# Inverse roots on the vector engine, another order in the wide attention layers, and filled gate chains

## What is computed

```python
x = x + L0_xattn(layernorm(x), ctx, ctx)      # "raw": 16 heads of 8, causal
x = x + L0_ffn(layernorm(x))                  # "ffn0": ternary weights, GELU
x = x + L1_xattn(layernorm(x), ctx, mask)     # "rows": 16 heads of 64, row mask
x = x + L1_ffn(layernorm(x))                  # "ffn1": batch norm, product keys, top 8
x = x + L2_xattn(ctx, layernorm(x))           # "bias": 16 heads of 8, causal, biases
x = x + L2_ffn(layernorm(x))                  # "ffn2": 8 experts, the best one, GELU
x = x + L3_xattn(layernorm(x), ctx, ctx, ...) # "keys": 16 heads of 64
x = x + L3_ffn(layernorm(x))                  # "ffn3": 8 experts, best two, + 2 shared ones
# layernorm(x) = (x - mean) / sqrt(var + 1e-5)
# shared part of ffn3: sh = silu(x @ ws_gate.T) * (x @ ws_up.T) @ ws_down.T
```

## Time and profile before

| what | us |
|---|---|
| median of 3 runs (lowest to highest) | 1647.35 (1647.21 to 1652.68) |
| profiled execution | 1640.3 |
| its span | 1638.5 |
| PE busy in the span | 1413.3 (86%) |
| DVE busy | 1022.6 (62%) |
| ACT busy | 898.7 (55%) |
| Pool busy | 690.4 (42%) |

### The profile page before, as it was taken

One profiled execution on the slowest core, in us unless ns is written; L12 is line 12 of the kernel. 1 busy time (PEld: TensorE's weight loads), 2 busy tenths in 40 slices (PEclk: granted clock), 3 DMA queues, 4 the chain that ended last, 5 costly groups with the idle time before them and its releaser, 6 DMA issues.

```text
span 1638.5 us, 30033 instructions
## 1 busy us (share of the span) xinstructions
PE 1413.3 (86%) x9437; PEld 937.4 (57%) x9449; DVE 1022.6 (62%) x3380; ACT 898.7 (55%) x1867; POOL 690.4 (42%) x1056
## 2 busy tenths in 40 slices
PE   5996889999998577868778895899899999996998
PEld 2443457777766476767654443444576777664343
DVE  5653366666665799998955554433566666655444
ACT  3665456666665477777746663333566666661222
POOL 5341144444443589989853331000344444441000
PEclk9999899999999689998999997999999999997999
DMA  2016000000000000000000000000000000000000
GB/s 66 17 49 252 4 4 5 3 3 3 3 3 1 26 1 1 1 0 0 1 1 1 1 2 1 26 1 0 4 4 4 3 3 6 0 1 1 7 6 13
DMA packets 12665, 21.76 MB, mean 13 GB/s; under 512 B 3088, under 2 KB 9120, under 8 KB 11936
## 3 DMA queue, kind: packets, MB, share of 16 engines
q1 hardware_dynamic: 12576, 20.63, 3.5%
HBM read 19.58 MB, written 1.05 MB: 13 GB/s over the span
## 4 chain that ended last, share of the span: by engine, by line
PE 61%; DVE 17%; ACT 12%; issue 8%; POOL 2%; DVEq 0%; ACTq 0%; DMA 0%; SPq 0%; POOLq 0%
PE bank L932 7%; PE bank L969 6%; PE bank L947 5%; DVE sb_both L1841 4%; PE bank L919 4%; ACT sb_both L1036 4%; PE bank L1880 3%; PE bank L2060 3%; PE bank L898 3%; PE bank L409 2%; PE bank L1888 2%; PE bank L451 2%; PE bank L1889 2%; PE bank L899 2%; PE bank L2130 2%
## 5 line engine op out<-in xcount | busy, mean ns | idle before, releaser
L1213 POOL TENSOR_TENSOR sb_both<-sb_both,sb_winv 128x512 f32<-128x512 f32 x256 | 260.8, 1040 | 323.7 <-DVE sb_winv L1143 323.7
L1036 ACT ACTIVATE sb_both<-sb_both,sb_wneg 128x256 f32<-128x256 f32 x512 | 253.0, 495 | 151.0 <-DVE sb_wneg L1137 150.9
L1768 POOL TENSOR_TENSOR sb_KM<-sb_OT 128x1024 f32<-128x1024 f32 x128 | 240.2, 1913 | 31.8 <-DVE sb_both L1841 27.8
L1672 PE MATMUL bank<-sb_ident,sb_both 128*128 128x128 f32 x1024 | 139.4, 286 | 59.3 <-DVE sb_both L1841 37.0
L1137 DVE CUSTOM_DVE_ANT_0 sb_both<-bank,sb_pen 128x256 f32<-128x256 f32 x512 | 182.1, 420 | 0.0
L1298 POOL TENSOR_TENSOR sb_ntmp<-sb_rstd 128x2 f32<-128x2 f32 (+2 forms) x123 | 24.2, 197 | 340.6 <-DVE sb_rstd L218 335.3
L1841 DVE SCALAR_TENSOR_TENSOR sb_both<-sb_KM,sb_best,bank 128x1024 f32<-128x1024 f32 x128 | 158.4, 1273 | 11.3 <-ACT bank L1743 11.3
L1672 PEld LDWEIGHTS bank<-sb_ident,sb_both 128*128 128x128 f32 x1024 | 119.2, 147 | 73.6 <-DVE sb_both L1841 47.4
L1743 ACT ACTIVATE bank<-sb_KM 128x1024 f32<-128x1024 f32 x128 | 129.6, 1023 | 35.3 <-DVE sb_both L1841 30.2
L947 PE MATMUL bank<-sb_ident,sb_both 128*128 128x128 f32 x1024 | 134.4, 274 | 12.2 <-DVE sb_QT L1150 12.1
L947 PEld LDWEIGHTS bank<-sb_ident,sb_both 128*128 128x128 f32 x1024 | 116.3, 141 | 36.0 <-issue 20.0
(11 more groups left out here) (273 smaller groups left out, 2731.0 us busy)
## 6 DMA issues: line engine op xcount, KB each, us to landing
sb_ctxT_in<-in_ctxT SPq DMA_DIRECT2D x24, 128.0 KB, 2.3
sb_F<-in_F SPq DMA_DIRECT2D x2, 1024.0 KB
sb_XO<-in_ctx SPq DMA_DIRECT2D x8, 128.0 KB, 2.0
sb_WKQ<-in_WKQ SPq DMA_DIRECT2D x1, 1024.0 KB, 9.0
sb_W1ALL<-in_ctxT SPq DMA_DIRECT2D x1, 1024.0 KB, 4.7
sb_xn_all<-in_keymask SPq DMA_DIRECT2D x1, 1024.0 KB, 4.3
out_x<-sb_x SPq DMA_DIRECT2D x4, 256.0 KB, 2.3
sb_x<-in_x SPq DMA_DIRECT2D x1, 896.0 KB, 4.7
```

The costliest lines, as they stand in the source:

```text
L1036: last = act.activation(p, p, ACT.Exp, scale=-1.0, bias=wneg[:, t % 4, h, i:i + 1], accum_out=wsum[:, t % 4, h, i:i + 1])
L1213: pool.tensor_tensor(p, p, winv[:, t % 4, :, i:i + 1].broadcast_to([P, 2, SEQ]), ALU.mult).then_inc(w_norm, 1)
L1672: last = pe.matmul(weight_bank(c), gated[:, h % 4, c * P:(c + 1) * P], ident[:], is_transpose=True, start=(h == 0 and c % 4 == 0), stop=(h ...
L1768: pool.tensor_tensor(dst, s[:, h, 0, :].unsqueeze(2).broadcast_to([P, NK, NK]), s[:, h, 1, :].unsqueeze(1).broadcast_to([P, NK, NK]), ALU. ...
```

## The change

1. Pool's `rsqrt` and the constant c15 go. `inverse_std` on DVE does the seed and behind it three rounds of three operations (square, times -0.5 veps, then "plus 1.5, times y" in one scalar_tensor_tensor), each waiting for the one before; LN_CHAIN is 10. It stands wherever `seed` stood, in DVE's queue.
2. Wide layers: PE's `out_product` goes into bank 7 behind the copies of queries and keys 4 and 5 of the batch; PE's wait for w_added moves to the queries of j=6. On DVE `copy_pt` of the even pair stands ahead of the second `inverses`, and `normalise(b + 1)` moves from u=2, ahead of the odd `copy_pt`, to u=1, behind it.
3. ffn2: all 16 up products of group 0 and their GELUs run in the gate chain, the Exp behind the fifth GELU, the gate's turn and its copy to gT behind the eleventh; their results lie in KM and VP. body(0) keeps bc, bias and down products.
4. ffn3: the two shared units leave the loop (8 units a group). Their work for all four groups (8 pairs of up products, 4 groups of down products, Silu and copies on ACT, products and the additions to x on Pool in `pool3`) is interleaved with the gate chain ahead of body(0).

```diff
-LN_CHAIN = 4 * NEWTON
+LN_CHAIN = 1 + 3 * NEWTON
...
-        def seed(dve, variance, lo, hi, at):
+        def inverse_std(dve, variance, lo, hi, at, ln):
+
+            v, bits, y, a = (t[:, lo:hi] for t in (veps, vbits, rstd, ntmp))
...
+            dve.tensor_scalar(y.bitcast(I32), bits, -1.0, RSQRT_SEED, ALU.mult, ALU.add).then_inc(newton_step, 1)
+            step = LN_CHAIN * ln
+            for k in range(NEWTON):
+                dve.wait_ge(newton_step, step + 3 * k + 1)
+                dve.tensor_tensor(a, y, y, ALU.mult).then_inc(newton_step, 1)
+                dve.wait_ge(newton_step, step + 3 * k + 2)
+                dve.tensor_tensor(a, a, vhalf[:, lo:hi], ALU.mult).then_inc(newton_step, 1)
+                dve.wait_ge(newton_step, step + 3 * k + 3)
+                dve.scalar_tensor_tensor(out=y, in0=a, scalar=1.5, in1=y, op0=ALU.add, op1=ALU.mult)\
+                   .then_inc(newton_step, 1)
...
+                if j == 6 and not known_below(b, 1):
+                    pe.wait_ge(w_added, A.batches + b)
...
-            def out_product(b, turned):
+            def out_product(b, copied):
                 pe.wait_ge(w_ot, heads(b + 1, 0))
-                pe.wait_ge(w_pt[1], A.pairs + turned)
+                pe.wait_ge(w_qk_out, A.pairs + copied)
...
-                        last = pe.matmul(bank[5][:, i * D:(i + 1) * D], OT[:, j, i * P:(i + 1) * P], WO[:, j, :],
+                        last = pe.matmul(bank[7][:, i * D:(i + 1) * D], OT[:, j, i * P:(i + 1) * P], WO[:, j, :],
...
-                    if t == 2 and i == 1 and not known_below(b, 1):
-                        pe.wait_ge(w_added, A.batches + b)
...
+                if behind or u >= 1:
+                    bt, ut = steps_back(b, u, 1)
+                    copy_pt(bt, 2 * ut)
                 inverses(b, 2 * u + 1)
...
-                if u == 2 and more:
-                    normalise(b + 1)
                 if behind or u >= 1:
                     copy_pt(bt, 2 * ut + 1)
+                if u == 1 and more:
+                    normalise(b + 1)
...
-                if u == 0 and part != "last":
-                    rsqrt(pool, 0, TPB, A.ln + b + 1, [0, 1])
-                if u == 1 and part != "last":
-                    rsqrt(pool, 0, TPB, A.ln + b + 1, [2])
...
-    UPS_AHEAD2, UNITS_AHEAD3 = 4, 2
+    EXP_AFTER2, GATE_AFTER2 = 4, 10
...
+    def shared_up(pe, q):
+
+        g, u = q // 2, q % 2
+        if q >= 2:
+            pe.wait_ge(sh_act, q - 1)
+        pe.matmul(bank[2 * u][:], SG[:, u, :], xnT_all[:, g * GROUP:(g + 1) * GROUP], start=True, stop=True)
+        pe.matmul(bank[2 * u + 1][:], SU[:, u, :], xnT_all[:, g * GROUP:(g + 1) * GROUP],
+                  start=True, stop=True).then_inc(sh_up, 1)
+
+    def shared_down(pe, g):
+
+        pe.wait_ge(sh_prod, 2 * g + 2)
+        if g >= 2:
+            pe.wait_ge(sh_out, g - 1)
+        for i in range(TPG):
+            for u in range(2):
+                last = pe.matmul(bank[4 + g % 2][:, i * P:(i + 1) * P],
+                                 gated_ring[:, (2 * g + u) % 4, i * P:(i + 1) * P], SD[:, u, :],
+                                 start=(u == 0), stop=(u == 1))
+        last.then_inc(sh_down, 1)
...
+        act.activation(act_ring[:, q % 4, :], bank[2 * u][:], ACT.Silu)
+        act.activation(shared_u[:, q % 4, :], bank[2 * u + 1][:], ACT.Copy).then_inc(sh_act, 1)
...
+        gate_logits(pe, A)
+        for n in range(16):
+            up2(pe, 0, n)
+            if n == GATE_AFTER2:
+                gate_turn(pe, A, 4)
+        pe.wait_ge(gT_ready, 2)
...
+                if known_zero(g) and n == EXP_AFTER2:
+                    gate_exp(act, A)
+                if known_zero(g) and n == GATE_AFTER2:
+                    gate_out(act, A, 4)
...
+        for q in range(4):
+            shared_up(pe, q)
+        gate_counts(pe)
+        shared_down(pe, 0)
+        shared_up(pe, 4)
+        shared_up(pe, 5)
+        shared_down(pe, 1)
+        gate_turn(pe, A, 6)
+        shared_up(pe, 6)
+        shared_up(pe, 7)
+        shared_down(pe, 2)
+        shared_down(pe, 3)
+        pe.wait_ge(gT_ready, 4)
+        pe.wait_ge(sh_out, GROUPS - 1)
```

More of the change, by code:

```diff
@@ L1120, in add_out @@
                 xb = x[:, bass.ds(TPB * b, TPB), :]
-                dve.tensor_tensor(xb, bank[5][:, 0:SEQ].rearrange("p (i d) -> p i d", i=TPB), xb, ALU.add)\
+                dve.tensor_tensor(xb, bank[7][:, 0:SEQ].rearrange("p (i d) -> p i d", i=TPB), xb, ALU.add)\
                    .then_inc(w_added, 1)
@@ L1883, in up3 @@
     def up3(pe, g, n):
-        if not (known_zero(g) and n < 2):
-            pe.wait_ge(prod_step, UNITS * g + n - 1)
-        wgate, wup, _ = unit_weights(n)
-        pe.matmul(bank[2 * (n % 2)][:], wgate, xnT_all[:, bass.ts(g, GROUP)], start=True, stop=True)
-        pe.matmul(bank[2 * (n % 2) + 1][:], wup, xnT_all[:, bass.ts(g, GROUP)],
-                  start=True, stop=True).then_inc(up_done[3], 1)
-    def gate_tensor(pe, A):
+        if known_zero(g) and n < 2:
+            pe.wait_ge(sh_act, 2 * GROUPS - 1 + n)
+        else:
+            pe.wait_ge(prod_step, EXPERTS * g + n - 1)
@@ new lines, in shared_evac, with pool3, product, add @@
+    def shared_evac(act, g):
+        act.wait_ge(sh_down, g + 1)
+        act.activation(shared_out[:, g, :], bank[4 + g % 2][:], ACT.Copy).then_inc(sh_out, 1)
+    def pool3(pool, A):
+        def product(q):
+            pool.wait_ge(sh_act, q + 1)
+            if q >= 4:
+                pool.wait_ge(sh_down, (q - 4) // 2 + 1)
+            pool.tensor_tensor(gated_ring[:, q % 4, :], shared_u[:, q % 4, :], act_ring[:, q % 4, :], ALU.mult)\
+                .then_inc(sh_prod, 1)
+        def add(g):
+            pool.wait_ge(sh_out, g + 1)
+            xg = x[:, TPG * g:TPG * g + TPG, :]
+            pool.tensor_tensor(xg, xg, shared_out[:, g, :].rearrange("p (i d) -> p i d", i=TPG), ALU.add)\
+                .then_inc(sh_added, 1)
+        for q in range(2 * GROUPS):
+            product(q)
+            if q >= 5 and q % 2 == 1:
+                add((q - 5) // 2)
+        add(GROUPS - 2)
+        add(GROUPS - 1)
@@ L1894, in gate_tensor, with gate_logits @@
+    def gate_logits(pe, A):
         k = A.index - 2
@@ L1922, in gate_tensor, with gate_exp, gate_out @@
                 last.then_inc(gT_done, 1)
[L1923 to L1925 removed]
+    def gate_exp(act, A):
+        act.wait_ge(gexp_go, A.index - 1)
+        act.activation(gt["e8"][:], gt["t1"][:], ACT.Exp).then_inc(gexp_done, 1)
+    def gate_out(act, A, first):
         k = A.index - 2
[L1927 to L1928 removed]
         for half_ in range(2):
             act.wait_ge(gT_done, 2 * k + half_ + 1)
[L1931 removed]
+            act.activation(gT[:, half_ * 1024:(half_ + 1) * 1024], bank[first + half_][:].bitcast(BF16), ACT.Copy)\
                .then_inc(gT_ready, 1)
@@ L2069, in body @@
                               start=True, stop=True).then_inc(bc_done[0], 1)
-                if not (known_zero(g) and n < UPS_AHEAD2):
+                if not known_zero(g):
                     up2(pe, g, n)
@@ L2092, in body @@
                 act.wait_ge(up_done[2], 16 * g + n + 1)
-                if not (known_zero(g) and n < 4):
+                if known_zero(g):
+                    to = first_acts[n]
+                else:
+                    to = act_ring[:, n % 4, :]
                     act.wait_ge(gated_done[0], 16 * g + n - 3)
-                act.activation(act_ring[:, n % 4, :], bank[n % 4][:], ACT.Gelu, bias=f1b[:, n:n + 1])\
-                   .then_inc(act_ready[2], 1)
+                act.activation(to, bank[n % 4][:], ACT.Gelu, bias=f1b[:, n:n + 1]).then_inc(act_ready[2], 1)
+                if known_zero(g) and n == EXP_AFTER2:
+                    gate_exp(act, A)
+                if known_zero(g) and n == GATE_AFTER2:
+                    gate_out(act, A, 4)
             act.wait_ge(down_done[0], 16 * g + 16)
@@ L2146, in body @@
                     down(g, n - 1)
-            down(g, UNITS - 1)
+            down(g, EXPERTS - 1)
         groups(pe, body)
@@ L2154, in scalar3 @@
         norm_scalar(act, A)
-        gate_scalar(act, A)
-        def body(g):
-            for n in range(UNITS):
-                act.wait_ge(up_done[3], UNITS * g + n + 1)
-                if not (known_zero(g) and n < 4):
-                    act.wait_ge(prod_step, UNITS * g + n - 3)
+        shared_act(act, 0)
+        shared_act(act, 1)
+        gate_exp(act, A)
+        shared_act(act, 2)
+        shared_act(act, 3)
+        shared_evac(act, 0)
+        shared_act(act, 4)
+        shared_act(act, 5)
+        shared_evac(act, 1)
+        gate_out(act, A, 6)
+        shared_act(act, 6)
+        shared_act(act, 7)
+        shared_evac(act, 2)
+        shared_evac(act, 3)
+        def body(g):
+            for n in range(EXPERTS):
+                act.wait_ge(up_done[3], EXPERTS * g + n + 1)
+                if known_zero(g) and n < 4:
+                    act.wait_ge(sh_prod, n + 5)
```

(4 more changed lines are left out.)

179 lines of the change are left out of this document (73 added, 106 removed).

## The result

The changed kernel took 1666.5 us in the median of five executions (1658.5 to 1675.7), against 1647.35 before (1646.96 to 1652.68 in five); the ratio is 1.0106, 95% interval 1.0080 to 1.0132. So it is slower, by 1.1%, and outside the range of 1635 to 1663.

What follows compares the result with a forecast made beforehand. PE was taken to set the pace, busy 37.99 of 39.89 us per wide batch. The terms summed to +1.5 us, added to the 1647.35 median for 1648.9; range 1635 to 1663.

Steps and rivals of the forecast that it cites:

- The price of a chain: On DVE behind the seed: nine dependent operations at 0.195 us each, 1.76 us for two tiles.
- Narrow layers: Raw and bias: chain delays PE's scores 1.07 us in 6 batches x 2 layers, +12.8; first batch's chain -1.2.
- Wide layers: Rows and keys: longer u=0 wait about offset by stalls removed, -0.8 us per layer, -1.6 in all.
- the terms 0.82, 0.70 and 0.1: Wide batch savings: u=1 output product's wait -0.82 us, u=2 wait for normalise -0.70, u=3 -0.1.
- The new chain puts the copy to 334.25 ...: PE +1.60: Wide layers, u=0: DVE's copy L1150 moves from 332.65 to 334.25, delaying PE's transposes by 1.60 us.
- Rival C: Wide steps' reordering returns only half of its two stalls: +0.75 x 14 = +10.5 us, 1659; chance 0.06.
- Rival B: All chains: a dependent DVE operation costs 0.25 us, not 0.195, giving 1663; chance 0.24.
- Hand-overs: Between layers: raw to ffn0 +0.95 us, rows to ffn1 +1.4, bias to ffn2 +1.55, keys to ffn3 +1.8.
- ffn2: First group: all 16 ups in the gate chain, downs end at 1062.8 against 1066.85, -4.0 us.
- rival D: Filled chains of ffn2 and ffn3: each new ACT table load costs a second 1.28 us, +3.8, 1653; chance 0.03.
- ffn3: Shared units out of the loop: three looped groups give 4.47 us each, start and group 0 +4.5; -10 taken.
- Before group 0 the shared units now stand in full: ffn3's gate chain takes 10.7 us of shared-unit PE work; first down product 29.9 us behind logits against 17.5, +12.4.

Runs made afterwards that it cites:

- e4: Changed kernel with the roots back on Pool, in wide layers all rounds in u=0, all else kept: 1601.9 us, ratio 0.970.
- e10: Kernel before with only the wide layers' new order, roots on Pool with all three rounds in u=0: 1615.3 us, ratio 0.978.
- e12: e4 plus nine dependent, useless DVE multiplications in u=0 of every wide batch: 1650.4 us.
- e7: Changed kernel, norm_stats moved to u=1 (wide) and behind maxima(n, 2) (narrow), ffn3's shared-unit Pool products cut to 32 columns: 1603.3 us, ratio 0.972.
- e1: Changed kernel with norm_stats and its nine root operations moved from u=0 to u=1 in the wide layers: 1620.9 us, ratio 0.981.
- e9: e4 with the wide loop's statistics, seed and nine root operations on DVE in u=1: 1603.1 us, ratio 0.971.

## Why the prediction was wrong, point by point

**The price of a chain** (1.76 us) was right: 0.195 apart, nine of them.

**Narrow layers**: +1.07 forecast, +1.15 measured (waits of 1.08 in six batches of raw and five of bias). The term of 12.8 should have been 13.8. The working had it: scores at 67.05 to 67.10 against 65.95 are 1.10 to 1.15 us, not 1.07. The first batch's own chain gave 1.5 (PE's first scores at 11.27 instead of 12.81) for 1.2. But the bias layer came out at +11.3 instead of +6.4. Ahead of its second batch's scores it had lost 4.9, of which the forecast has at most one chain's 1.07; another 1.9 belong to the hand-over below. There PE's first wait for a reduction grew too, from 1.32 to 2.48, and behind it PE ran 17 us at half clock (3.4 before); the last row is of 15 of them:

```profile
863.27 1.14 PE L415 MATMUL bank<-sb_QT,sb_outT 32*128 32x512 f32 x8 [2.48 <-DVE sb_VP L698]
...
866.00:881.00 15.00, 12.03 (x43) 5.94 (x44) 5.56 (x9) 3.95 (x7) 4.79 (x9) 0.50 0.00 0
```

Whether this wait causes it stays open. With one round, and in e4 and e10 with Pool's roots, there is no such stretch in that batch; with two rounds (a wait of 1.89) there are 17 us; but e12, whose roots are on Pool and whose wait there is 1.32 us as before, has one of 14 us too.

**Wide layers**: the time was wrong: -1.6 for both layers, -2.6 with the hand-overs into them, and with these +10.8 measured. In a looped batch the new order gave 2.00 us (e10, 37.89 against 39.89) where the terms 0.82, 0.70 and 0.1 gave 1.62, and the chain took 1.69 (39.58 against 37.89) where 1.60 was forecast. Both were near. The step that failed is "The new chain puts the copy to 334.25 ...: PE +1.60". It priced a longer wait of PE at its length. Waits of 0.42, 0.78 and 0.70, three per batch and 1.90 in sum, were traded for one of 2.16, and the one long wait has a second price, 1.62 us at the lower clock, eleven times here, 17.8 us. (The looped batches' other 0.3 and shorter layer ends took 7 back.) It could have been read in the trace of before, at the one long wait of PE in each wide layer's last batch (timeline of PE, kernel before; the 16 products L969 take 1.9 us elsewhere):

```profile
522.26 1.06 PE L947 MATMUL bank<-sb_ident,sb_both 128*128 128x128 f32 x8 [2.35 <-DVE sb_QT L1150]
524.12 3.33 PE L969 MATMUL bank<-sb_QT,sb_VP 128*64 128x256 f32 x16 [0.79 <-DVE sb_QT L1150]
```

The text speaks of PE's half clock in ffn2 and ffn3 and never asks it of the wide layers. Rival C puts the same place at up to +10.5, but by a wait that came back; none did. Rival B, the likeliest on the slower side, named a dearer operation, 0.25 us; they stand 0.195 apart.

**Hand-overs**: rows to ffn1 as told. The memset starts at once and holds veps:

```profile
548.59 3.51 POOL L855 MEMSET sb_VP<- 128x4096 f32 x1 [12.10 <-DVEq L1208]
...
549.42 2.71 DVE L211 TENSOR_SCALAR sb_veps<-sb_mv 128x2 f32<-128x2 f32 x1
554.27 4.19 DVE L1468 TENSOR_SCALAR sb_xn_all<-sb_x,sb_mv,sb_rstd 128x128 f32<-128x128 f32 x16
```

The tiles are over 9.98 us behind the last addition instead of 9.02, +0.96 for +1.4. Keys to ffn3: the first tile 3.28 behind the addition instead of 1.51, +1.77 for +1.8. Bias to ffn2 can't be read from the last addition, since the chain for 14 tiles stands ahead of it in DVE's queue and moves it: PE's product for it is over at 1035.21, and the addition follows at 1040.69, right behind the chain.

```profile
1034.50 0.71 PE L392 MATMUL bank<-sb_WO,sb_XO 128*128 128x128 f32 x4 [0.47 <-ACT sb_XO L641]
...
1040.60 0.17 DVE L224 SCALAR_TENSOR_TENSOR sb_rstd<-sb_ntmp,sb_rstd 128x14 f32<-128x14 f32 x1
1040.69 0.42 DVE L675 TENSOR_TENSOR sb_x<-bank,sb_x 128x256 f32<-128x256 f32 x1
```

From the end of the addition before that, the tiles take 14.4 us instead of 13.2: +1.2 for +1.55. In the table 1.9 of it stand in the bias row, and -0.7 in ffn2's.

**ffn2**: -3.3 for -4.0, no more than what the same group differs by between executions. ACT's table loads in the filled chain:

```profile
1061.45 1.28 ACT L1960 ACT_TABLE_LOAD   x1
1062.75 0.31 ACT L1960 ACTIVATE sb_g_e<-sb_g_t 128x128 f32<-128x128 f32 x1
1063.07 1.28 ACT L2137 ACT_TABLE_LOAD   x1
1064.37 1.84 ACT L2137 ACTIVATE sb_KM<-bank,sb_f1b 128x512 f32<-128x512 f32 x3
```

The next activation starts 0.02 us behind each load, so rival D falls (ffn3's load for the Exp is the same: 1.28 us from 1542.84, the Exp at 1544.13). The Trainium skill (ScalarE: Activation LUTs, What ACT_TABLE_LOAD costs) gives a drain of some 1380 ns on top; this trace doesn't show one.

**ffn3**: the three looped groups gave what was forecast (-4.55 each for -4.47). The first group with its hand-over cost +11.05 where the sum had +4.5 +1.8, less 1.1 for the clock, or +5.2. Two mechanisms were missing from the step "Before group 0 the shared units now stand in full". Pool's products hold DVE's gate operations, 0.29 becoming 1.2 to 1.4 (e7: 4.0 us of the tail, some 2 of the group). The row for it stood in the forecast, used for one memset only. And PE waits 5.00 us at the hand-over instead of 3.23, and the 32 logits behind it take 6.83 us instead of 3.82:

```profile
1525.02 4.10 PE L1475 MATMUL bank<-sb_ident,sb_xn_all 128*128 128x128 f32 x16 [5.00 <-DVE sb_xn_all L1468]
1528.92 6.83 PE L1934 MATMUL bank<-sb_gateW,sb_xnT_all 128*128 128x8 f32 x32
```

I had expected the filled chain to keep the clock up and took 1.1 us for that; it began at half clock, and of the first group with its hand-over 17 us ran at half clock against 20 before.

**The base.** The terms were read in a profiled execution of 1640.3 us and added to a median 7 us above it. Had all of the trace's differences been known (+27), the forecast from the median would have been 1674, 8 above what was measured. The two traces differ in more than the change does, and by which stages isn't shown.

## What to carry to other kernels

Moving work to a faster engine pays or costs by what stands behind it in that engine's queue: the same nine operations of the wide layers, in u=0, make the kernel 3% slower than in u=1 (e1), where they cost nothing against Pool's (e9 against e4). Before such a move look for the place where the engine waits for the bottleneck anyway (here DVE waits 4.3 to 4.6 us at one place of each batch, in both kinds of layers). And price a wait of PE not by its length alone: add up where short waits are traded for one long one, and read the granted clock behind waits of that length elsewhere in the same trace.
